# An expert layer's second product, split into three products of high and rest parts

## The reference, cut to what matters

```python
routes = argmax(softmax(xt @ Wr + br))
h = gelu(xt @ W1[e] + b1[e])        # 256 -> 1024, exact gelu
y = h @ W2[e] + b2[e]               # 1024 -> 256
t = t + y * (routes == e)
```

## Time and profile before

| | us |
|---|---|
| median of 3 runs | 1265.84 |
| lowest and highest | 1262.71, 1266.04 |
| the profiled execution's own time | 1267.67 |
| its span, first to last instruction | 1265.8 |
| PE busy in the span | 1149.1 (91%) |
| DVE, ACT, POOL busy in the span | 675.9, 406.5, 584.2 |

### The profile page before, as it was taken

One profiled execution on the slowest core, in us unless ns is written; L12 is line 12 of the kernel. 1 busy time (PEld: TensorE's weight loads), 2 busy tenths in 40 slices (PEclk: granted clock), 3 DMA queues, 4 the chain that ended last, 5 costly groups with the idle time before them and its releaser, 6 DMA issues. The chain is left out here.

```text
span 1265.8 us, 23320 instructions
## 1 busy us (share of the span) xinstructions
PE 1149.1 (91%) x7492; PEld 824.5 (65%) x7493; DVE 675.9 (53%) x1509; ACT 406.5 (32%) x465; POOL 584.2 (46%) x570
## 2 busy tenths in 40 slices
PE   5899999897679999999999999988944999999995
PEld 3577677575255555555555555547834999999994
DVE  3265546445557777777777777715842333333331
ACT  1303231310115555555555555552210111111110
POOL 0003030201117888887787888880252444444443
PEclk8799999898679999999999999999956999999998
DMA  6204252213151334333232334236626656656551
GB/s 205 59 1 125 105 182 83 114 49 151 67 191 40 102 82 112 79 93 100 67 100 67 102 80 112 44 118 205 202 89 179 210 187 196 210 191 204 202 190 60
DMA packets 96119, 156.81 MB, mean 124 GB/s; under 512 B 44848, under 2 KB 65264, under 8 KB 94416
## 3 DMA queue, kind: packets, MB, share of 16 engines
q1 hardware_dynamic: 87728, 130.20, 33.4%
q0 software_dynamic: 7536, 22.96, 5.5%
q10 hardware_dynamic: 816, 3.15, 0.7%
HBM read 108.77 MB, written 44.06 MB: 121 GB/s over the span
## 5 line engine op out<-in xcount | busy, mean ns | idle before, releaser
L217 DVE TENSOR_REDUCE s_nmax<-h_ps_m 128x1 f32<-128x512 f32 x484 | 311.4, 685 | 116.7 <-PE h_ps_m L211 106.7
L925 POOL TENSOR_TENSOR h_added<-h_added,h_expd 128x1024 f32<-128x1024 f32 x128 | 304.9, 2382 | 38.7 <-ACT h_expd L948 30.2
L948 ACT ACTIVATE h_expd<-h_ps_e 128x1024 f32<-128x1024 f32 x256 | 248.2, 1021 | 153.9 <-PE h_ps_e L967 150.5
L1616 PEld LDWEIGHTS ps_h<-xs_c,lnt 128*128 128x128 f32 x1248 | 147.0, 194 | 4.8 <-issue 2.9
L1616 PE MATMUL ps_h<-xs_c,lnt 128*128 128x128 f32 x1248 | 147.4, 277 | 2.3 <-DVE xs_c L1568 2.3
L418 POOL TENSOR_TENSOR a_res<-a_res,a_lnt 128x2048 f32<-128x2048 f32 x4 | 18.2, 4538 | 267.9 <-DVE a_lnt L123 267.9
L1626 PE MATMUL ps_y<-w,vals_t 128*128 x624 | 141.2, 379 | 0.6 <-DVE ys L1581 0.6
L981 PE MATMUL h_ps_o<-h_expd,s_vh 128*32 128x256 f32 x2048 | 137.2, 385 | 0.6 <-ACT h_expd L948 0.6
L580 PE MATMUL a_ps_v<-a_val,a_expd 128*128 128x257 f32 x512 | 121.2, 391 | 5.1 <-ACT a_expd L458 4.5
L1626 PEld LDWEIGHTS ps_y<-w,vals_t 128*128 128x128 f32 x624 | 115.5, 190 | 15.1 <-issue 1.0
L1657 ACT ACTIVATE vals_t<-ps_h 128x1024 f32<-128x1024 f32 x39 | 40.0, 1024 | 260.8 <-DVE ps_h L1561 260.8
(11 more groups left out here) (194 smaller groups left out, 1479.0 us busy)
## 6 DMA issues: line engine op xcount, KB each, us to landing
lnt<-in_w SPq DMA_DIRECT2D x39, 1024.0 KB, 4.8
qk_scr<-a_head_hi SPq DMA_DIRECT2D x16, 512.0 KB, 2.7
qk_scr<-a_head_lo SPq DMA_DIRECT2D x16, 512.0 KB, 3.6
w<-in_w SPq DMA_DIRECT2D x8, 1024.0 KB, 5.8
xs<-xs_scr SPq DMA_DIRECT2D x39, 128.5 KB, 2.0
a_x_t<-in_x_t POOLq DMA_DIRECT2D x4, 1024.0 KB, 10.0
r_scr<-a_res POOLq DMA_DIRECT2D x4, 1024.0 KB, 5.9
v_scr<-res SPq DMA_DIRECT2D x4, 1024.0 KB, 3.9
```

Source lines behind the costliest of these rows:

```text
L217: self.nc.vector.tensor_reduce(self.nmax[k][:, nb, half:half + 1], ps_m[:, half, :], AX.X, ALU.max, negate=True).then_inc(self.v_max, 1)
L925: nc.gpsimd.tensor_tensor(total[:, :], (expd[:, 0, :] if m == 1 else total[:, :]), expd[:, m, :], ALU.add).then_inc(g_add, 1)
L948: nc.scalar.activation(expd[:, m, :], flat(ps_e[m % 2]), ACT.Exp, scale=SCALE).then_inc(a_exp, 1)
L1616: last = nc.tensor.matmul(ps_h[k][:, c // 4, c % 4 * P:(c % 4 + 1) * P], w1_now[k][:, t, c * P:(c + 1) * P], xs_c[:, t, :], start=(t == 0) ...
```

## The change

The second layer is computed as three F32R products for each of the eight blocks of hidden units: high units by high weights, high units by the rest of the weights, rest of the units by high weights. ScalarE writes the high part of a tile's weights (`weights_hi`, a copy of 128x2048 elements from `w2` into F32R) and of its units (the gelu written as F32R). It then writes the gelu once more, in place in PSUM in F32, and VectorE takes the rests as differences (`weights_lo`, 128x2048, both inputs in SBUF; `units_lo`, 128x1024, one input in PSUM). `ps_y` gets a second buffer, so that the second layer of tile i waits for the result of tile i - 2 and no longer of i - 1 (`v_ys` starts at one through a small memset, and POOL's wait is raised by one to match).

```diff
-        hid_t = [keep["vals_t"][:, k, :, :] for k in range(2)]
+        hid_hi, hid_lo = ([sb(f"hid_{x}{k}", [P, KC, P], F32R) for k in range(2)] for x in ("hi", "lo"))
+        w2_hi, w2_lo = ([sb(f"w2_{x}{k}", [P, KC, C], F32R) for k in range(2)] for x in ("hi", "lo"))
...
-        ps_x, ps_y = ps("ps_x", [P, HALF]), ps("ps_y", [P, HALF])
+        ps_x, ps_y = ps("ps_x", [P, HALF]), [ps(f"ps_y{k}", [P, HALF]) for k in range(2)]
...
-                    pool.wait_ge(v_ys, i + 1)
+                    pool.wait_ge(v_ys, i + 2)
...
+                nc.vector.memset(ys[:, 0:1], 0.0).then_inc(v_ys, 1)
...
+                def weights_lo(i, k, first=False):
+
+                    e = expert(i)
+                    dve.wait_ge(a_whi, i + 1)
+                    if not first:
+
+                        dve.wait_ge(pe_ys, i - 1)
+                    nc.vector.tensor_tensor(w2_lo[k][:, :, :], w2[:, bass.ds(e, 1)].rearrange("p o k n -> p (o k) n"),
+                                            raw(w2_hi[k][:, :, :]), ALU.subtract).then_inc(v_wlo, 1)
+
+                def units_lo(i, k, first=False):
+
+                    dve.wait_ge(a_gelu, i + 1)
+                    if not first:
+
+                        dve.wait_ge(pe_ys, i - 1)
+                    nc.vector.tensor_tensor(hid_lo[k][:, :, :].rearrange("p k n -> p (k n)"), flat(ps_h[k]),
+                                            raw(hid_hi[k][:, :, :]).rearrange("p k n -> p (k n)"), ALU.subtract).then_inc(v_hlo, 1)
...
                     if ahead:
                         tokens(i + 2)
-                    result(i, first)
+                    if next_tile:
+                        weights_lo(i + 1, 1 - parity, first)
+                        units_lo(i + 1, 1 - parity, first)
+                    result(i, parity, first)
...
                 tokens(0)
+                weights_lo(0, 0, first=True)
                 biased(0, 0)
+                units_lo(0, 0, first=True)
                 tokens(1)
...
                     if not first:
-                        pe.wait_ge(a_gelu, i - 1)
+                        pe.wait_ge(v_hlo, i - 1)
...
                 def second_layer(i, k, first=False):
-                    e = pe.value_load(texp_i[0:1, bass.ds(i, 1)], min_val=0, max_val=E - 1)
                     if not first:
                         pe.wait_ge(v_ys, i)
-                    pe.wait_ge(a_gelu, i + 1)
+                    pe.wait_ge(v_wlo, i + 1)
+                    pe.wait_ge(v_hlo, i + 1)
                     for c in range(KC):
-                        last = nc.tensor.matmul(ps_y[:, 0:C], hid_t[k][:, c, :],
-                                                w2[:, bass.ds(e, 1), c, :].rearrange("p o n -> p (o n)"),
-                                                start=(c == 0), stop=(c == KC - 1))
+                        for h, w in ((hid_hi, w2_hi), (hid_hi, w2_lo), (hid_lo, w2_hi)):
+                            last = nc.tensor.matmul(ps_y[k][:, 0:C], h[k][:, c, :], w[k][:, c, :],
+                                                    start=(c == 0 and (h, w) == (hid_hi, w2_hi)),
+                                                    stop=(c == KC - 1 and h is hid_lo))
...
+                def weights_hi(i, k, first=False):
+                    e = act.value_load(texp_i[0:1, bass.ds(i, 1)], min_val=0, max_val=E - 1)
+                    if not first:
+
+                        act.wait_ge(pe_ys, i - 1)
+                    nc.scalar.activation(w2_hi[k][:, :, :], w2[:, bass.ds(e, 1)].rearrange("p o k n -> p (o k) n"),
+                                         ACT.Copy).then_inc(a_whi, 1)
...
-                    nc.scalar.activation(hid_t[k].rearrange("p k n -> p (k n)"), flat(ps_h[k]), ACT.Gelu).then_inc(a_gelu, 1)
+                    nc.scalar.activation(hid_hi[k][:, :, :].rearrange("p k n -> p (k n)"), flat(ps_h[k]), ACT.Gelu).then_inc(a_hhi, 1)
+                    act.wait_ge(a_hhi, i + 1)
+                    nc.scalar.activation(flat(ps_h[k]), flat(ps_h[k]), ACT.Gelu).then_inc(a_gelu, 1)
```

More of the change, by code:

```diff
@@ L1387, in expert_phase @@
         pe_xs, pe_hid, pe_ys = sem("pe_xs"), sem("pe_hid"), sem("pe_ys")
-        a_gelu = sem("a_gelu")
+        a_hhi, a_gelu, a_whi = sem("a_hhi"), sem("a_gelu"), sem("a_whi")
+        v_hlo, v_wlo = sem("v_hlo"), sem("v_wlo")
         all_consts = 16 * len(TABLE_CONSTS)
@@ L1568, in tokens, with result @@
                     nc.vector.tensor_copy(xs_c[:, :, :], ps_x[:, 0:C].rearrange("p (t n) -> p t n", t=CT)).then_inc(v_xs, 1)
-                def result(i, first=False):
+                def weights_lo(i, k, first=False):
[11 more added lines that the diff above has]
+                                            raw(hid_hi[k][:, :, :]).rearrange("p k n -> p (k n)"), ALU.subtract).then_inc(v_hlo, 1)
+                def result(i, k, first=False):
                     e = expert(i)
@@ L1580, in result @@
                     dve.wait_ge(v_rows, i + 1)
-                    nc.vector.tensor_tensor(ys[:, :], ps_y[:, 0:C], t_rows[:, :], ALU.add).then_inc(v_ys, 1)
+                    nc.vector.tensor_tensor(ys[:, :], ps_y[k][:, 0:C], t_rows[:, :], ALU.add).then_inc(v_ys, 1)
                 def tile(i, parity=0, first=False, next_tile=True, ahead=True):
@@ L1656, in gelu @@
                         act.wait_ge(pe_ys, i - 1)
-                    nc.scalar.activation(hid_t[k].rearrange("p k n -> p (k n)"), flat(ps_h[k]), ACT.Gelu).then_inc(a_gelu, 1)
+                    nc.scalar.activation(hid_hi[k][:, :, :].rearrange("p k n -> p (k n)"), flat(ps_h[k]), ACT.Gelu).then_inc(a_hhi, 1)
+                    act.wait_ge(a_hhi, i + 1)
+                    nc.scalar.activation(flat(ps_h[k]), flat(ps_h[k]), ACT.Gelu).then_inc(a_gelu, 1)
                 def tile(i, parity=0, first=False, next_tile=True, ahead=True):
                     if next_tile:
+                        weights_hi(i + 1, 1 - parity, first)
                         gelu(i + 1, 1 - parity, first)
+                act.wait_ge(v_experts, 1)
+                act.wait_ge(sems["w_in"], 16 * E)
+                weights_hi(0, 0, first=True)
                 gelu(0, 0, first=True)
```

## The result

The changed kernel takes **1307.01 us** (median, 1302.93 to 1312.36) against 1265.94 us of the kernel before in the same rounds (1262.71 to 1270.38). The ratio is 1.0325, 95% interval 1.0295 to 1.0355: slower by 41 us. Forecast were 1259.0, with 1250 to 1276 as the range. The prediction is wrong in sign and by 48 us.

The account below looks back on a forecast made before the run. TensorE was taken to bound the kernel before, the long loop through `ys` after. A 13.3 us gain less 3.6 and 1.2 at the start and 1.7 at the end gave -6.8, so 1259.0 us, range 1250 to 1276.

Parts of the forecast that it names:

- GpSimd's indirect DMAs keep their pace while VectorE reads two SBUF tiles: On GpSimd: DMAs take 0.97 us beside such passes, 0.98 where VectorE is idle, so the sum leaves GpSimd as it is.
- the gather's loop of 6.4 us: From the end of `ys` through the gather to the next tile's: 5.4, 0.56 and 0.42 us, not changed.
- the second rival: On TensorE: F32R products of 256 columns cost what those of 512 do, loop 9.4 us, kernel 1350; chance 0.08.
- also the gather stops for `weights_lo`: On GpSimd: the gather waits 2.3 us on a loop of 6.4, +34, kernel 1300; within a shared chance of 0.08.
- The first rival: On GpSimd: small steps stop while `weights_lo` runs, 1.2 to 1.6 us once in three tiles, kernel 1274; chance 0.20.
- Level from 0.6 us of hold on: GpSimd's small steps held about 0.6 us: with the losses at both ends the kernel is level.
- The period: Distance between tiles, set by the largest loop: 6.88 us, 0.37 less than before, a gain of 13.3 us.
- The loop from `ys` of tile i to that of i + 3: Through GpSimd, SP's loads, first layer and VectorE: 20.6 us, 6.88 a tile, longer than TensorE's 6.6.
- 2.8, from half of 233 ns: TensorE's second layer: 24 F32R products of 256 columns at 117 ns, 2.8 us in place of 3.46.
- 5.78: VectorE's chain from the bias to the end of `ys`: 5.78 us, fitting under TensorE's 6.6 us.
- start 4.8 forecast: At the start: tile 1's first layer 3.6 us later, and 1.2 us lost to a low TensorE clock.
- The longer way to `ys` at the end: Last tiles: `ys` of tile 37 is 5.35 us behind the last first layer, 3.66 before; 1.7 us lost.

Follow-up runs that it names:

- e8: The changed kernel with the subtraction of the weights in two passes of 1024 elements in place of one of 2048; ratio 1.0112, median 1281.73 us.
- e1: The changed kernel with the second input of the weights' subtraction taken from zeros in PSUM, same length, output off; ratio 0.9957, median 1263.88 us.
- e3: The changed kernel with the result of tile i between the two subtractions, ahead of that of the units; ratio 1.0064, median 1276.57 us.
- e4: The kernel before with an unused 128x2048 subtraction, both inputs in SBUF, on VectorE behind each tile's result; ratio 1.0299, median 1308.10 us.
- e2: The changed kernel with the subtraction of the weights cut into eight passes of 256 elements; ratio 1.0031, median 1273.12 us.
- e10: e6 with the weights' subtraction as one pass whose second input is zeros in PSUM, so not the real rest; ratio 0.9843, median 1250.15 us.
- e7: The kernel before with an unused 128x2048 subtraction behind each result, one input being zeros in PSUM; ratio 0.9990, median 1267.25 us.
- e5: The changed kernel with the result between the two subtractions and that of the weights in eight passes of 256 elements; ratio 0.9923, median 1258.54 us.
- e6: e5 with the copy of tile 1's tokens ahead of the units' subtraction of tile 0 at the start; ratio 0.9885, median 1253.31 us.

## Why the prediction was wrong

**The step that failed** is the one on GpSimd: "GpSimd's indirect DMAs keep their pace while VectorE reads two SBUF tiles", "So the sum leaves GpSimd as it is", and of the gather's loop of 6.4 us, "That loop is not changed". The runs showed in its place: a gather whose start falls into the pass stands until the pass ends, 1.5 to 2.0 us in each tile, and it stands in the one loop that had been counted as fixed. 6.4 + 2.0 = 8.4 and 6.4 + 1.5 = 7.9, and about 8.4 and 7.9 in turn are the distances that the `ys` keep.

**Why misled.** They show a VectorE pass with two SBUF inputs at 950.69 and a DMA at 950.66. The DMA was first, by 0.03 us. e8 shows that this is the harmless order, and that it turns over within 0.1 us. The next DMA, at 951.93, came after the pass had ended. The rows never held the case that the change makes, a GpSimd instruction that starts inside such a pass, and the test was taken as passed on two rows. In the whole trace before, none starts inside a pass with two SBUF inputs that has more than 0.26 us left. In e1's trace VectorE's preparation lies 1.8 us later against the same DMAs, and one of them starts 0.04 us inside a pass of 0.48 us with both inputs in SBUF:

```profile
949.36 0.48 DVE L1544 TENSOR_TENSOR tiled<-tile_no,end 128x312 f32<-128x312 f32 x1
949.40 1.28 POOL L1107 DMA_INDIRECT xs_scr<-lnt,pos  x1 [0.30 <-issue]
```

It takes 1.28 instead of 0.97 us. The Trainium skill (SBUF — State Buffer, "SBUF: two separate sides") describes an exclusive lock that whichever of the two starts first keeps for the whole instruction; by that rule, the runs agree as far as GpSimd is the one that waits: 37 gathers of 39, and the additions of e3 and e4. In the other direction the runs don't show it: in e3, 17 passes began while a gather was running and took 2.28 to 2.29 us, as ever, and in e8 the longest of 34 such halves took 1.29 in place of 1.22.

**The rivals.** The case had been named, at the end of the second rival: "also the gather stops for `weights_lo`: 2.3 us on a loop of 6.4 give about 8, +34, 1300". That is what happened, by mechanism, place and nearly size (8.1, +41, 1307). The size is partly luck: "about 8" was not worked out (2.3 on 6.4 would be 8.7), since the part of the pass that was left at the gather's start was not estimated, and of the +34 the distances were 27, where they came to 33.75. The case shared a chance of 0.08 with the one that it was put beside, since the earlier trace rows "speak against it". The first rival (small steps held, 1274) was true as a mechanism, and hidden in the changed kernel; e3 laid it open. Level from 0.6 us of hold on, the forecast had said; e2, with holds of some tenths in the gather, the additions and the copy, came out 0.3% slower than before, but its eight pieces also take 0.5 us a tile longer than the one pass, so it doesn't test that figure by itself.

**The other terms** held, most of them as e1 shows them, the changed kernel without the hold:

- The period: 6.88 forecast, 6.91 measured over 38 distances (6.99 where 6.66, 6.66 and 7.64 repeat). The loop from `ys` of tile i to that of i + 3 ties the kernel as described, with TensorE waiting for `lnt<-in_w`.
- TensorE: e10's bare distance is 6.66 us; less 3.57 and 0.22 it leaves 2.87 for the second layer, 24 x 120 ns. Forecast were 2.8, from half of 233 ns.
- VectorE: `w_lo` 2.28 us (2.30), `hid_lo` 1.22 (1.23 busy, 1.14 as a step). From the bias at 1073.11 in e1 to the end of `ys` at 1078.88 are 5.77 us; forecast were 5.78.
- In the changed kernel itself: start 4.8 forecast, 4.85 measured. The longer way to `ys` at the end: 1.7 forecast; `ys` of tile 37 starts 5.21 us behind the end of the last first layer in e1 and 3.49 before, 1.72 more.
- The sum of all, without a hold: -6.8 forecast; e1's ratio is -0.43%, -5.4. In its trace the 38 distances give -11.8 of the -13.3, and the first `ys` is 7.9 us late, where 6.5 were forecast. That is -3.9 in this one execution; the difference to -5.4 is within what single executions differ by (1259.0 to 1267.1).

So one step was wrong and the other terms held. It weighed as much as it did because it decided not a term but which loop ties: by the ratios, 47 us lie between e1 and the changed kernel.

## What to carry to other kernels

- A new long VectorE pass with both inputs in SBUF is charged to GpSimd as well. Look in the trace for what GpSimd starts in that stretch, and add the pass's rest to the loop that contains it. Eight passes of 256 elements took away about four fifths of it (e2: +0.3% in place of +3.2%, and -0.4% without any hold). One input in PSUM took all of it away (e1, e7), but here that input was zeros; no run puts a real operand there.
- A row shows that two engines don't disturb each other only if it has the order that the change makes. Read which one was first, to the hundredth, before it is used as evidence, and then set the chance by how many such rows there are.
- Price the slack loops with the same care as the one that ties. Here they lay close together (6.4, 6.6 and 6.88 us), and 1.5 to 2.0 us missing in the slackest outweighed every entry of the others. Moving one call and cutting one pass (e5), and then moving one more call (e6), turned +3.2% into -1.2% with the same arithmetic.

## What the runs showed of the hardware that I had not expected

- The hold is at the start of a GpSimd instruction, whatever its size: one element a partition (2.29 for 0.19 us, e3) or an indirect DMA (2.96 for 0.98). The DMA ends 0.86 us behind the pass, so all but 0.12 us of its 0.98 come after the hold; the addition ends 0.06 behind it.
- It turns over between 0.02 us ahead and 0.08 us behind the pass's start (e8). Two other traces narrow that: gathers that started 0.025 us behind the first piece went free in 0.98 us (e5, e6), and one 0.036 behind took 1.24 (e2). For the `pause` additions the border lies a little earlier: in e3, three that started 0.016 to 0.021 us ahead of the pass took 0.19, and one 0.005 ahead took 2.34. With a pass cut in pieces it ends with the running piece, though the pieces follow each other without a gap.
- F32R products of 256 columns follow each other by 120 ns, 24 in 2.87 us, where those of 512 take 233: at these two widths the time goes by the columns.
- TensorE's clock at the start. The windows of 977 to 983 us (columns as in the first such row), of e1 and of e6:

```profile
977.00:983.00 6.00, 6.00 (x34) 6.00 (x34) 0.36 (x1) 0.00 (x0) 0.00 (x0) 0.59 0.02 10
```

```profile
977.00:983.00 6.00, 6.00 (x54) 6.00 (x53) 5.78 (x13) 3.85 (x3) 0.46 (x3) 1.00 0.68 223
```

The granted clock is 0.59 on the mean in e1, so most of these 6 us lie at the lower of its two levels (1.2 GHz), and 1.00, the 2.4 GHz level, in e6. Ahead of tile 1's first layer TensorE had been idle for 4.99 us in e1 and 1.63 in e6. After the same 4.99 us the layer took 5.28 us in the changed kernel, 5.83 in e5 and 6.72 in e1, against 3.81: the loss isn't a fixed sum, it lay between 1.5 and 2.9 us. The forecast's 1.2 was near the lower end, so that the start came out right (4.85 for 4.8) is partly luck: e1 has the same order and lost 2.9.
